# Split products and an earlier context product in the tail of a decoder layer

## The reference

```
# x: (4, 512, 512), ctx: (4, 512, 256), all float32; 16 heads of 128
x = x + attn(layernorm(x))            # gated delta-rule scan over 16 heads, then out @ Wout
x = x + xattn(layernorm(x), ctx)
x = x + ffn(layernorm(x))

def xattn(t, f):
    query = einsum('bnc,dc->bnd', f, Wq) + bq          # 'context' products
    key   = einsum('bnc,dc->bnd', f, Wk) + bk
    attention = softmax(einsum('bnd,bmd->bnm', query, key))
    return einsum('bln,bmn->blm', t, attention)        # 'attended'

def ffn(t):                                            # E = 8 experts of rank R = 64
    gate = argmax(softmax(t @ Wg.T)); p = its probability
    h = einsum('nd,erd->ner', t, A) * one_hot(gate)    # 'up'
    return einsum('ner,eor->no', h, Bw) * 4.0 * p      # 'down'
```

## Time and profile before

| | us |
|---|---|
| median of three runs | 2014.83 |
| profiled execution, its time | 2019.99 |
| its span | 2018.3 |
| TensorE busy in the span | 1908.4 (95%) |
| tail, from the first product behind the heads | 1572.71 to 2018.3 |
| first out product of batch 1 | 1693.75 |
| first out product of batch 3 | 1909.89 |

### The profile page before, as it was taken

The page is one execution under the profiler, slowest core; times in us unless marked ns, Lnnn a source line. Parts: engine busy times, 40 slices in busy tenths (PEclk is TensorE's granted clock), DMA queues, the critical chain, the costliest instruction groups (busy, mean ns, idle before and its releaser), DMA issues.

```text
span 2018.3 us, 45513 instructions
## 1 busy us (share of the span) xinstructions
PE 1908.4 (95%) x16962; PEld 1558.9 (77%) x16962; DVE 1128.2 (56%) x2048; ACT 933.0 (46%) x2987; POOL 743.3 (37%) x1143
## 2 busy tenths in 40 slices
PE   6899999999999999999999999999997799999999
PEld 4688888888888888888888788888887565656574
DVE  6656566565657465655657574656564352524333
ACT  2556464646455555646465655546463221213121
POOL 1345363645445353636264544536361000000000
PEclk9899899999989899989999998999897899999999
DMA  3011111201021111112020111111113503121200
GB/s 117 6 33 40 25 37 28 43 22 38 22 42 29 32 40 25 34 25 44 21 43 22 38 30 35 40 24 36 25 30 145 156 21 94 42 84 52 61 23 21
DMA packets 220198, 87.12 MB, mean 43 GB/s; under 512 B 138320, under 2 KB 204240, under 8 KB 219280
## 3 DMA queue, kind: packets, MB, share of 16 engines
q1 hardware_dynamic: 220048, 84.83, 16.6%
HBM read 57.28 MB, written 27.53 MB: 42 GB/s over the span
## 4 chain that ended last, share of the span: by engine, by line
PE 60%; issue 21%; DVE 9%; ACT 5%; POOL 4%; DMA 1%; POOLq 0%; DVEq 0%; SPq 0%; ACTq 0%
PE bank L562 27%; PE bank L871 4%; DVE vT L1383 3%; PE bank L821 3%; PE bank L830 2%; PE bank L783 2%; PE bank L772 2%; PE bank L691 2%; PE bank L815 2%; ACT vv L1084 2%; PE bank L837 1%; PE bank L934 1%; PE bank L952 1%; PE bank L669 1%; PE bank L659 1%
## 5 line engine op out<-in xcount | busy, mean ns | idle before, releaser
L562 PE MATMUL bank<-x_hi,w_hi 128*128 128x512 f32 x1024 | 429.8, 420 | 14.7 <-DVE vT L1383 14.3
L562 PE MATMUL bank<-x_hi,w_lo 128*128 128x512 f32 x1024 | 408.9, 399 | 1.8 <-issue 1.8
L562 PE MATMUL bank<-x_lo,w_hi 128*128 128x512 f32 x1024 | 406.5, 397 | 0.0
L562 PEld LDWEIGHTS bank<-x_hi,w_hi 128*128 128x128 f32 x1024 | 196.0, 191 | 55.6 <-issue 13.4
L562 PEld LDWEIGHTS bank<-x_hi,w_lo 128*128 128x128 f32 x1024 | 195.7, 191 | 45.6 <-issue 2.2
L562 PEld LDWEIGHTS bank<-x_lo,w_hi 128*128 128x128 f32 x1024 | 196.6, 192 | 32.0 <-issue 0.6
L1383 DVE SCALAR_TENSOR_TENSOR qT<-bank,cw,qT 128x511 f32<-128x511 f32 (+2 forms) x192 | 142.1, 747 | 51.0 <-ACT qT L1033 46.5
L1848 POOL TENSOR_TENSOR rstd<-ve,mhalf 128x1 f32<-128x1 f32 x32 | 17.4, 544 | 390.2 <-DVE ve L1607 390.2
L1216 ACT ACTIVATE o_tmp<-bank 128x128 f32<-128x128 f32 x256 | 67.4, 278 | 179.0 <-PE bank L837 179.0
L1383 DVE SCALAR_TENSOR_TENSOR vT<-bank,cw,vT 128x511 f32<-128x511 f32 (+2 forms) x192 | 143.0, 745 | 8.6 <-ACT vT L1033 4.1
L1383 DVE SCALAR_TENSOR_TENSOR kT<-bank,cw,kT 128x511 f32<-128x511 f32 (+2 forms) x192 | 143.4, 747 | 5.0
(11 more groups left out here) (221 smaller groups left out, 4447.3 us busy)
## 6 DMA issues: line engine op xcount, KB each, us to landing
w_raw<-in_w_heads SPq DMA_DIRECT2D x64, 256.0 KB, 2.8
o_d<-og SPq DMA_DIRECT2D x64, 256.0 KB, 2.6
o_raw<-o_d SPq DMA_DIRECT2D x16, 1024.0 KB, 6.2
x_in<-in_x SPq DMA_DIRECT2D x16, 256.0 KB, 3.6
blkN_d<-nT SPq DMA_DIRECT2D x64, 64.0 KB, 2.0
t<-blkT_d SPq DMA_DIRECT2D x64, 64.0 KB, 2.4
wo_raw<-in_w_out SPq DMA_DIRECT2D x4, 1024.0 KB, 9.5
x_res<-in_x SPq DMA_DIRECT2D x16, 256.0 KB, 2.8
```

The source lines that it names most:

```text
L562: last = mm(bank[bk][:, :], w[:, kind % 2, d, :], xx[:, d, b * S:(b + 1) * S], start=(n == 0), stop=(n == 3 * ND - 1))
```

## The change

The products of `attended`, `up` (without the gate columns) and `down` go from four f32 products each to twelve float32r ones. For this VectorE subtracts a low part for every transposed chunk, straight from PSUM (`ln_low`, `att_low`, `hm_low`); ScalarE's copies become the high parts, and in stage 1 it copies twice (`xfT` in f32 for the gate, `xfT_hi`). In batch 0 `a_sb` and `b_sb` are split too. To make room, `o_lo` now lies on `o_raw`, in place, so that `load_heads` has to wait for the product of two chunks earlier (`oproj_mm`); `xlT` has three buffers for four chunks, `xfT` two. The context products of batch b+1 stand behind `attended(3)` of batch b, ahead of `ln_transpose(1, 1)`. Batch 3 is written out on TensorE.

```
     a_lo = at(place["a_sb"][0], "a_lo", ...); b_lo = at(place["b_sb"][0], "b_lo", ...)
     o_lo = at(place["o_raw"][0], "o_lo", [P, 2, H, P], F32R)
...
# sync
-                        sp.wait_ge(olo_done, t - 1)
+                        sp.wait_ge(oproj_mm, t - 1)
...
# tensor: attended
-                    for k in range(ND):
-                        last = mm(bank[c % 2][:, :], xlT[:, c, k, :], attT[:, k, :], start=(k == 0), stop=(k == ND - 1))
+                    for k in range(ND):
+                        mm(bank[c % 2][:, :], xlT_hi[:, c % 3, k, :], attT_hi[:, k, :], start=(k == 0), stop=False)
+                    pe.wait_ge(lnT_low, 8 * b + c + 1)
+                    for k in range(ND):
+                        mm(bank[c % 2][:, :], xlT_lo[:, c % 3, k, :], attT_hi[:, k, :], start=False, stop=False)
+                    if c == 0:
+                        pe.wait_ge(attT_low, 4 * b + 4)
+                    for k in range(ND):
+                        last = mm(bank[c % 2][:, :], xlT_hi[:, c % 3, k, :], attT_lo[:, k, :], start=False, stop=(k == ND - 1))
# up and down: hi x hi and hi x lo by k, a wait for the low part, then lo x hi
...
# tensor: order of a batch
                 if first:
-                    context()
+                    context(0)
...
                 else:
                     out_product(0)
-                    context()
                     energy(0)
...
                 attended(3)
+                if more:
+                    context(b + 1)
                 ln_transpose(1, 1)
                 ln_transpose(1, 2)
...
# tensor: ln_transpose(stage, c), n = 4 * stage + c
                     if n >= 2:
                         pe.wait_ge(lnT_done, 8 * b + n - 1)
+                        pe.wait_ge(lnT_low, 8 * b + n - 1)
...
# scalar
                 def ln_copy(stage, c):
                     act.wait_ge(lnT_mm, 8 * b + 4 * stage + c + 1)
-                    fn((xlT, xfT)[stage][:, c, :, :], grid(2 + c % 2), ACT.Copy).then_inc(lnT_done, 1)
+                    if stage == 0:
+                        if c == 3:
+                            act.wait_ge(xm_mm, 4 * b + 1)
+                        fn(xlT_hi[:, c % 3, :, :], grid(2 + c % 2), ACT.Copy).then_inc(lnT_done, 1)
+                    else:
+                        act.wait_ge(h_mm, 4 * b + max(c - 1, 0))
+                        fn(xfT[:, c % 2, :, :], grid(2 + c % 2), ACT.Copy)
+                        fn(xfT_hi[:, c % 2, :, :], grid(2 + c % 2), ACT.Copy).then_inc(lnT_done, 1)
...
# vector
+                def ln_low(stage, c):
+                    dve.wait_ge(lnT_done, 8 * b + 4 * stage + c + 1)
...
+                        dve.wait_ge(h_mm, 4 * b + max(c - 1, 0))
+                    tt(low, grid(2 + c % 2), high.bitcast(F32), ALU.subtract).then_inc(lnT_low, 1)
```

More of the change, by code:

```diff
@@ L197, in layer @@
     att = tk("att", [P, NC, S])
+    o_lo = at(place["o_raw"][0], "o_lo", [P, 2, H, P], F32R)
+    hmT_hi = at(place["att"][0], "hmT_hi", [P, 2, ND, P], F32R)
+    hmT_lo = at(place["hmT_hi"][1], "hmT_lo", [P, 2, ND, P], F32R)
+    assert place["hmT_lo"][1] <= place["att"][1]
     assert tk.end <= place["vT"][0]
@@ L204, in layer @@
     kx = tl("kx", [P, S])
-    attT = tl("attT", [P, NC, S])
+    attT_hi = tl("attT_hi", [P, NC, S], F32R)
+    hm = at(place["attT_hi"][0], "hm", [P, 2, D])
+    attT_lo = tl("attT_lo", [P, NC, S], F32R)
     x_res = tl("x_res", [P, NC, D])
     xl = tl("xl", [P, 2, D])
[L208 to L212, removed]
+    xlT_hi = tl("xlT_hi", [P, 3, ND, P], F32R)
+    xlT_lo = tl("xlT_lo", [P, 3, ND, P], F32R)
+    xfT = tl("xfT", [P, 2, ND, P])
+    xfT_hi = tl("xfT_hi", [P, 2, ND, P], F32R)
+    xfT_lo = tl("xfT_lo", [P, 2, ND, P], F32R)
+    a_hi = tl("a_hi", [P, ND, E * R], F32R)
+    b_hi = tl("b_hi", [P, E * R // P, D], F32R)
     t_small = Plan(consts_end)
@@ L486, in _ @@
             head(H - 1, False, False)
-            for s in heads_over:
-                sp.wait_ge(s, 1)
+            sp.wait_ge(heads_over, 4)
             for s in og_out:
@@ L846, in _, with batch, context @@
             pe.wait_ge(og_done, 4 * H)
-            mm(bank[0][:, 0:2], ident[:, :], ident[:, 0:2], start=True, stop=True).then_inc(heads_over[PE_], 1)
+            mm(bank[0][:, 0:2], ident[:, :], ident[:, 0:2], start=True, stop=True).then_inc(heads_over, 1)
             pe.wait_ge(t_consts, 16 * 7)
             pe.wait_ge(wo_lo_done, 4)
[L850 to L854, removed]
+            def batch(b, first, more):
+                def context(of):
+                    pe.wait_ge(ctx_in, 16 * of + 16)
+                    pe.wait_ge(attT_low, 4 * of)
                     pe.wait_ge(y_done, 4 * b)
@@ L950, in down @@
                         pe.wait_ge(y_done, 4 * b + c - 1)
+                    elif more:
+                        pe.wait_ge((qx_done, kx_done)[c], b + 2)
                     for k in range(E * R // P):
-                        last = mm(bank[4 + c % 2][:, :], hmT[:, c % 2, k, :], b_sb[:, k, :],
-                                  start=(k == 0), stop=(k == E * R // P - 1))
+                        mm(bank[4 + c % 2][:, :], hmT_hi[:, c % 2, k, :], b_hi[:, k, :], start=(k == 0), stop=False)
+                        mm(bank[4 + c % 2][:, :], hmT_hi[:, c % 2, k, :], b_lo[:, k, :], start=False, stop=False)
+                    pe.wait_ge(hmT_low, 4 * b + c + 1)
+                    for k in range(E * R // P):
+                        last = mm(bank[4 + c % 2][:, :], hmT_lo[:, c % 2, k, :], b_hi[:, k, :],
+                                  start=False, stop=(k == E * R // P - 1))
                     last.then_inc(y_mm, 1)
                 if first:
-                    context()
+                    context(0)
                     energy(0)
@@ L998, in batch @@
                 down(3)
-            batch(0, True)
-            with pe.Fori(1, B) as b:
-                batch(b, False)
+            batch(0, True, True)
+            with pe.Fori(1, B - 1) as b:
+                batch(b, False, True)
+            batch(B - 1, False, False)
         @block.scalar
@@ L1251, in _, with batch @@
             o_split(0, 1)
-            def batch(b, more):
+            def batch(b, first, more):
                 def exponentials(m):
@@ L1281, in batch @@
                 o_split(b, 3)
+                if first:
+                    fn(a_hi[:, :, :], a_sb[:, :, :], ACT.Copy).then_inc(ab_hi_done, 1)
+                    fn(b_hi[:, :, :], b_sb[:, :, :], ACT.Copy).then_inc(ab_hi_done, 1)
                 ln_copy(0, 1)
@@ L1293, in batch @@
                 ln_copy(1, 0)
+                if more:
+                    context(b + 1)
                 ln_copy(1, 1)
-                ln_copy(1, 2)
                 def hm_copy(c):
@@ L1305, in route @@
                        accum_out=ex_sum[:, c:c + 1]).then_inc(rt_exp, 1)
+                ln_copy(1, 2)
+                route(0)
                 ln_copy(1, 3)
-                route(0)
                 route(1)
@@ L1574, in o_split, with batch @@
                 tt(o_lo[:, c % 2, :, :], o_raw[:, c % 2, :, :], o_hi[:, c % 2, :, :].bitcast(F32), ALU.subtract).then_inc(olo_done, 1)
-            for s in heads_over:
-                dve.wait_ge(s, 1)
+            dve.wait_ge(heads_over, 4)
             o_split(0, 0)
             o_split(0, 1)
-            def batch(b, more):
+            def batch(b, first, more):
                 def maximum(m):
@@ L1627, in batch @@
                 maximum(3)
+                ln_low(0, 0)
                 o_split(b, 3)
@@ L1632, in batch @@
                 layernorm(0, 1)
+                if first:
+                    for i, (low, raw, high) in enumerate(((a_lo, a_sb, a_hi), (b_lo, b_sb, b_hi))):
+                        dve.wait_ge(ab_hi_done, i + 1)
+                        tt(low[:, :, :], raw[:, :, :], high[:, :, :].bitcast(F32), ALU.subtract).then_inc(ab_lo_done, 1)
+                ln_low(0, 1)
+                att_low(0)
+                att_low(1)
                 residual(0, 2)
@@ L1637, in batch @@
                 residual(0, 3)
+                att_low(2)
+                att_low(3)
                 layernorm(0, 3)
+                ln_low(0, 2)
+                ln_low(0, 3)
+                residual(1, 0)
+                layernorm(1, 0)
                 if more:
                     o_split(b + 1, 1)
-                for c in range(NC):
+                for c in (1, 2):
                     residual(1, c)
                     layernorm(1, c)
+                ln_low(1, 0)
+                residual(1, 3)
+                layernorm(1, 3)
+                ln_low(1, 1)
+                ln_low(1, 2)
                 def route(c):
@@ L1671, in result @@
                     dve.wait_ge(y_store[c % 2], 32 * b + 16 * (c // 2))
-                    tt(y_out[:, c % 2, :], x_res[:, c, :], bank[4 + c % 2][:, :], ALU.add).then_inc(y_done, 1)
+                    tt(y_out[c % 2][:, :], x_res[:, c, :], bank[4 + c % 2][:, :], ALU.add).then_inc(y_done, 1)
```

(11 more changed lines are left out.)

86 lines of the change are left out of this document (59 added, 27 removed).

## The result

The changed kernel takes 1987.82 us (median of 4 runs, 1979.97 to 1991.44) against 2013.53 (4 runs): ratio 0.9868, 95% interval 0.9828 to 0.9908. The forecast was 1990, range 1975 to 2002.

The account below looks back on a forecast made before the run. TensorE's order was taken to bound the tail. Products -33.6, waits that go -12.6, waits that come +17.0 and clock +5.1 sum to -24.1 us; from the 2014.8 median that gives 1990.7, called 1990, range 1975 to 2002.

Parts of the forecast that it names:

- The products: In `attended`, `up` and `down`, 48 groups of twelve float32r products would each save 0.70 us: -33.6 us.
- Waits that go: TensorE's waits ahead of `attended(2)` (-5.9), the energies (-2.8) and a transpose (0.5), plus slow clock (-3.4), vanish: -12.6 us.
- Waits that come: New TensorE waits: `ln_transpose(0,0)` 7.9, `attended(3)` 4.6, batch 3's `ln_transpose(1,2)` 2.3, `expert_transpose(0)` 2.2; sum +17.0 us.
- The rival of the reload chain: `o_raw` loads landing in 9.5 us lengthen waits at `ln_transpose(0,0)`, other chunks and `attended(3)`: 2041 us, chance 0.05.
- The clock: Three of eight new TensorE waits of 1.5 us and more bring the 1.2 GHz level, 1.7 us each: +5.1 us.

Follow-up runs that it names:

- second split late: Changed kernel with VectorE's `o_split(b+1,1)` moved from ahead of `residual(1,1)` to behind `ln_low(1,1)`: 1975.36 us, ratio 0.9799, tail 412.4 us.
- its repeat: The changed kernel run again with nothing changed: 1980.80 us, ratio 0.9846, tail 419.4 us.
- residual first: Changed kernel with `residual(0,0)`, `attention(0)`, `attention(1)` and `layernorm(0,0)` ahead of `o_split(b,2)` on VectorE: 1990.23 us, ratio 0.9905, tail 413.6 us.
- context products back: Changed kernel with the context products and their copies back behind `out_product(0)`: 2005.26 us, ratio 0.9966, tail 436.2 us.

## Why the prediction was right

- *The products.* -33.6 forecast. The distances give 0.66 for `up` with its gate columns (4.33 to 3.67), 0.58 to 0.70 for `attended`, 0.70 for `down`: about -32. The term missed that a float32r group behind f32 transposes or f32 gate columns takes 0.12 more (2.85 against 2.73). The Trainium skill (FP8 and Floating Point Precision, TensorE Precision Notes) has true f32 as four passes. An estimate from that, three quarters of the old cost for three split products, would have saved 0.86 each. The trace does not bear the estimate out: 2.73 to 2.85 is 0.80 to 0.83 of 3.43.
- *Waits that go.* -12.6, and all of it went: `attended(2)`, the energies and the transpose have no row, and the two slow stretches behind the old waits are gone.
- *Waits that come.* +17.0 forecast, +14.7 measured, term by term: 7.9 and 6.7 (batches 2 and 3 have their `xl` 0.2 earlier than forecast, and TensorE comes 0.2 later), 4.6 and 4.0, 2.3 and 2.3, 2.2 and 1.7. The rival of the reload chain had the right place; its price needed a landing of 8 us, and the slowest was 6.3.
- *The clock.* +5.1 as three stretches of 1.7; there were two, of 1.4 and 3.1, 4.5 in all. That the sum came so close is in part luck: one stretch fewer, and one that was twice as long as the rows of 1.7 that the price came from (3.4 us lost by its stretches; with the second split late, the same work at the same place lost 1.7).
- *Not in the sum.* Batch 0's first energies wait 5.1 instead of 6.8. In the other kernels this row is 4.9 to 6.5, so it isn't put down to the change.

Together -32.0 - 12.6 + 14.7 + 4.5 - 1.7 = -27.1, beside -26.7 in the tail. The forecast of -24.1 was thus small by 2.6, with every term within 2.5 of what it measured. For the profiled execution the forecast was 1995.9 and it came out at 1979.97, 15.9 less: 13.3 of that lies in the heads. The medians are 25.7 us apart where the forecast was tested and 31.4 on the second chip (2012.23 and 1980.80), beside 26.7 and 26.2 in the tails; that the first comes so near the tail's owes something to luck, since runs of the changed kernel alone differ by up to 18 us.

## What to carry to other kernels

Where one engine's list bounds a stretch, make its products cheaper and at once ask which other engine's list it now reaches too early: here 32 us of cheaper products gave 21, and another 20 us came off the changed kernel's tail when the other lists were put in order. An item that needs a late load should stand in its engine's list behind everything that doesn't, and independent work (here the next batch's context products) should stand where the other engine is latest. When kernels share a long part that varies, compare the stretch that was changed, not the spans.

## What the runs showed of the hardware

- The clock behind TensorE's waits of over 1 us, over the nine profiles (the tail behind its first energies): after 28 waits of 1.04 to 1.62 us it never fell; after ten of 1.97 to 2.33 it fell six times; after eight of 2.71 to 3.27 it fell every time. The Trainium skill (TensorE: Matmul & The Clock Gate, What's actually happening) says of the warm-up that the point where the clock changes varies from run to run. No two runs here show that for the fall: the changed kernel and its repeat fell behind the same two waits. From place to place and from kernel to kernel it does vary: of three waits of 1.97 in one run of the kernel before, two brought it, and batch 3's wait of 2.3 brought it in the changed kernel, its repeat, residual first and second split late, and not with the context products back.
- Runs of one program differ by up to 18 us (1977.62 to 1995.93 for the changed kernel), with the mean granted clock beside it: 0.969 and 0.959 for these two. The kernel before spans 20 us on one chip (2005.56 to 2025.93, 0.968 and 0.957).
- With its clock up, TensorE starts float32r products of 128x512 0.227 us apart and takes 3.43 us for four plain f32 ones, so twelve split products (2.73 us) cost 0.80 of the four that they stand for, and 0.83 (2.85 us) behind f32 work.
